# A one-core kernel of a two-layer selective-scan tower, attention and a quantised feed-forward: the later stages' steps placed inside the last iterations of the scan loop

## The chip, the cores and the metric

The kernel runs on one core of one Trainium2 chip. The metric is the device time of the program in microseconds (us), smaller is better. Before the change three runs took 442.88, 443.31 and 444.84 us; their median is 443.31. One more execution was profiled, and every row below is from that one.

## The reference, cut to what matters

Sixteen sequences of 128 tokens, 192 features each, fp32. Three stages follow one another, each with a residual:

```python
x = emb[input_ids]                                # (16, 128, 192)
for i in range(2):                                # selective scan block, inner width 384, 16 states
    x = x + mamba_block(rmsnorm(x, norm_w[i]), ...)
#   in mamba_block: xz = x @ in_proj_w; causal convolution of 4 taps, silu; x_dbl = xr @ x_proj_w;
#   delta = softplus(dt @ dt_proj_w + dt_proj_b); scan over the tokens; (y * silu(res)) @ out_proj_w
h = x
#   attention, 12 heads of 16: weights relu(1 + s + s*s/2) with s = q.k/4, divided by their sum
h = h + attention(layernorm(h)) @ w_proj + b_proj
#   feed-forward, 192 -> 2*512 -> 192: input and hidden are rmsnormed and rounded to 8 bits per token
#   (scale 127 / largest magnitude), weights rounded to -1, 0, 1; y = silu(gate) * up
h = h + bitlinear(y, w_out, g_out)
```

## The kernel before

The five engines run queues of their own and meet only at semaphores; the kernel is written by hand as one list of operations for each engine. A wait stands in the queue, so everything behind it on that engine waits too.

**The scan loop.** Work goes in eight chunks: two layers (`NL`) by four groups of four sequences (`NG`, `SG`), a chunk being 512 token columns, and the 384 inner channels three tiles `c` of 128 partitions. On each engine `for i in range(NJ + 5)` runs a software pipeline, in which iteration `i` handles different steps of chunks `i-1` to `i-5`. In the last iterations (`i` from 10 on) no new chunk comes in and the steps get fewer: `project_out(7, b)` of TensorE (L709) and `add_h(7, b)` of VectorE (L1273) end the loop. `gate(j, c)` (L1261) multiplies by the gate and releases `project_out(j)`. VectorE's part of a chunk is the convolution (L1172), `error` (L1164), `delta` (L1179), `input_times_b` (L1194), `memoryless_states` (L1208), the scan (L1200), `skip` (L1213), `times_c` (L1219). Whether the slower recurrence over 15 further states is needed is decided by a flag (L1266) that each engine reads (`states_*`); with these inputs the branch is not taken.

**Attention and feed-forward.** They start after the loop. `variances(g)` (L1280, L1283, L1285) of groups 0 to 2 stand in the last iterations of VectorE's loop, that of group 3 behind it; `normalise(s)` (L1369) follows. Per group of four sequences: `turn_x` (eight transposes, L763), `take_x` (L458, L461), `project_qk` twice (L776, L781), `take_q` and `take_k` (L470, L1376), `sum_tokens` (L1391), `sum_values` (L810), `project_v` (L792, L797), `take_v` (L1383). Per sequence, on TensorE: `scores` (L822), `values` (L836), `turn_sums` (L845), `turn_attention` (L851), `project` (L859), then of the feed-forward `turn_input` (L868), `project_up` (L882), `turn_hidden` (L891), `project_down` (L899). A second loop, `for i in range(SEQ + 6)`, issues one turn per sequence: attention of sequence `i` beside `project_up(i-3)`, `turn_hidden(i-4)` and `project_down(i-5)`. Between these steps ScalarE squares the scores (L478) and copies or applies silu (L487, L494, L501, L510, L516, L522), VectorE divides (L1406, L1411), adds (L1417) and finds the largest magnitudes (L1434, L1457), and GpSimd multiplies by the gain (L1044) and makes the scales.

**Banks and buffers.** There are eight PSUM banks. The loop uses 0 and 1 for transposes and for `project_out`, 2 to 7 for the rest. After it, the scores take 0 to 2, the pair 3 and 4 (`U_BANK`) holds in turn what `turn_x`, `project_qk`, `project_v` and `project_up` make, 5 is for values, 6 for attention, 7 for the feed-forward. The buffers of attention and feed-forward are views of the loop's buffers `pair` (xc, sz), `dl`, `du`, `arena` and `ring`; `pair`, `dl` and `du` are laid out with the channel tile outside and the chunk inside.

## Time and profile before

| | |
|---|---|
| median of 3 runs | 443.31 us |
| the profiled execution: its time | 447.74 us |
| its span, first to last instruction | 445.9 us |
| TensorE matmul busy | 382.3 us (86%), 1794 instructions |
| TensorE weight load busy | 203.9 us (46%) |
| VectorE busy | 324.2 us (73%) |
| ScalarE busy | 304.5 us (68%) |
| GpSimd busy | 202.0 us (45%) |
| mean granted TensorE clock | 0.891 of full speed |

Span and time differ by 1.84 us of start and end. The shares are means over stages with different limits: the scan loop (to about 259 us), the handover (to about 294), and attention with feed-forward. A matmul's end is modelled in the trace, since matmuls overlap; the distance between the starts of two steps is the safer measure.

### The profile page before, as it was taken

To read this page: it belongs to the slowest core of one execution; us is meant where nothing else is said; L and a number is where in the kernel's file an instruction comes from. 1 tells how busy PE (TensorE), PEld (TensorE's weight loads), DVE (VectorE), ACT (ScalarE), POOL (GpSimd) and SP (SyncE) were. 2 spreads that over 40 slices of the span, in tenths; PEclk is the share of its full clock that TensorE was granted. 3 is DMA by queue.
4 is the path that set the end of the run, shared out by engine and by line. 5 is a ranking of instruction groups with operands and counts; after the bars stand their busy time and mean duration, and the time that the engine had idled before them with its cause. 6 is when DMAs were issued, how large, how long until landed. Compare 5 with 4: busy or idle time off the path is not lost. (4 is left out here: it accounts for less than half of the span.)

```text
span 445.9 us, 6460 instructions
## 1 busy us (share of the span) xinstructions
PE 382.3 (86%) x1794; PEld 203.9 (46%) x1794; DVE 324.2 (73%) x687; ACT 304.5 (68%) x574; POOL 202.0 (45%) x298
## 2 busy tenths in 40 slices
PE   0489989999999999999887656989899999998853
PEld 0233333363444535445262551544665765665522
DVE  2079897999999999999979965134486477557752
ACT  1268997999999899998987002166296477558532
POOL 5546525355344543635254422002366445647772
PEclk9997895999999999999986666899699889989865
DMA  6832000000000000000000000000000000000000
GB/s 145 236 91 54 1 1 0 1 1 1 1 2 0 1 0 2 1 1 1 0 0 2 0 1 0 2 0 1 2 10 10 11 10 19 9 12 20 10 18 26
DMA packets 6877, 7.88 MB, mean 18 GB/s; under 512 B 1566, under 2 KB 5623, under 8 KB 6840
## 3 DMA queue, kind: packets, MB, share of 16 engines
q1 hardware_dynamic: 5238, 5.71, 4.6%
q0 software_dynamic: 768, 1.57, 1.6%
q8 instruction: 16, 0.26, 0.3%
q10 hardware_dynamic: 834, 0.17, 0.2%
q14 instruction: 21, 0.17, 0.1%
HBM read 5.87 MB, written 1.57 MB: 17 GB/s over the span
## 5 line engine op out<-in xcount | busy, mean ns | idle before, releaser
L583 PE MATMUL bank<-ring,win 96*128 96x512 f32 x192 | 101.4, 671 | 2.0 <-issue 1.2
L583 PEld LDWEIGHTS bank<-ring,win 96*128 96x128 f32 x192 | 37.4, 208 | 57.8 <-issue 52.0
L983 POOL TENSOR_TENSOR du<-dl,pair 128x512 f32<-128x512 f32 x24 | 30.9, 1289 | 71.8 <-DVE dmin L1179 71.8
L1172 DVE SCALAR_TENSOR_TENSOR pair<-bank,cw,pair 128x508 f32<-128x508 f32 (+2 forms) x72 | 52.2, 734 | 10.9 <-ACT pair L312 9.0
L709 PE MATMUL bank<-wout,pair 128*128 128x192 f32 x192 | 41.4, 376 | 5.9 <-DVE pair L1261 5.9
L709 PEld LDWEIGHTS bank<-wout,pair 128*128 128x128 f32 x192 | 37.1, 221 | 16.6 <-issue 9.1
L988 POOL TENSOR_TENSOR arena<-arena 128x512 f32<-128x512 f32 x24 | 30.6, 1274 | 30.9 <-DVE arena L1213 30.9
L977 POOL TENSOR_TENSOR arena<-arena,dl 128x512 f32<-128x512 f32 x24 | 30.5, 1269 | 14.8 <-DVE dl L1164 14.8
L478 ACT ACTIVATE pair<-bank 128x512 f32<-128x512 f32 x48 | 25.2, 597 | 11.1 <-PE bank L822 10.5
L637 PE MATMUL bank<-dbl,wdt 13*128 13x512 f32 x48 | 28.4, 675 | 4.6 <-issue 1.3
L1200 DVE TENSOR_TENSOR_SCAN arena<-arena 128x512 f32<-128x512 f32 x24 | 29.1, 1212 | 0.0
L312 ACT ACTIVATE pair<-bank,cb,cw 128x512 f32<-128x512 f32 x24 | 18.6, 774 | 13.6 <-PE bank L583 13.4
L1044 POOL TENSOR_TENSOR arena<-ring,gout 128x512 f32<-128x512 f32 x16 | 20.3, 1271 | 15.9 <-issue 10.1
L470 ACT ACTIVATE pair<-bank,parity 96x512 f32<-96x512 f32 x16 | 10.1, 678 | 22.1 <-PE bank L781 14.5
L620 PE MATMUL bank<-pair,wx 128*80 128x512 f32 x48 | 22.2, 599 | 2.3 <-ACT pair L346 2.2
L501 ACT ACTIVATE du<-bank,neg_rne 96x256 bf16<-96x256 f32 x16 | 7.5, 468 | 23.9 <-PE bank L868 23.9
L573 PE MATMUL bank<-ident,ring 128*96 128x128 f32 x64 | 9.2, 291 | 16.1 <-DVE ring L1150 16.1
L1179 DVE CUSTOM_DVE_ANT_0 dl<-du,arena 128x512 f32<-128x512 f32 x24 | 20.2, 843 | 1.4 <-ACT du L342 0.8
L342 ACT ACT_TABLE_LOAD x16 | 20.5, 1283 | 0.3
L959 POOL DMA_INDIRECT h<-emb,idx x16 | 17.7, 1108 | 6.0 <-issue 4.3
L776 PE MATMUL bank<-arena,wa 128*96 128x512 f32 x32 | 16.9, 655 | 3.0 <-ACT pair L470 1.6
L1164 DVE SCALAR_TENSOR_TENSOR dl<-du,dl 128x512 f32<-128x512 f32 x24 | 17.6, 734 | 2.5 <-ACT du L337 2.4
(161 smaller groups left out, 879.4 us busy)
## 6 DMA issues: line engine op xcount, KB each, us to landing
out<-h SPq DMA_DIRECT2D x16, 96.0 KB, 1.6
win<-in_w SPq DMA_DIRECT2D x2, 576.0 KB
arena<-ffn_in_t SPq DMA_DIRECT2D x1, 768.0 KB
wout<-out_w SPq DMA_DIRECT2D x2, 288.0 KB
arena<-ffn_out_t SPq DMA_DIRECT2D x1, 384.0 KB
wa<-w_qkv SPq DMA_DIRECT2D x1, 288.0 KB
wb<-w_qkv SPq DMA_DIRECT2D x2, 144.0 KB
h<-emb,idx POOLq DMA_INDIRECT x16, 6.9
```

The source lines that it names most:

```text
L342: nc.scalar.activation(du[:, c, j % NG, :], du[:, c, j % NG, :], ACT.Ln).then_inc(ln_done, 1)
L478: nc.scalar.activation(sq[:, s % 2, r, :], bank[:, r, :], ACT.Square, scale=HD ** -0.5, bias=1.0).then_inc(sq_ready, 1)
L583: last = nc.tensor.matmul(bank[:, b, :], win[:, j // NG, k, m * P:(m + 1) * P], xtr[:, j % 2, k, :], start=(k == 0), stop=(k == KH - 1))
L620: last = nc.tensor.matmul(bank[0:XM, XP_BANK, :], wx[:, j // NG, c, :], xc[:, c, j % NG, :], start=(c == 0), stop=(c == CI - 1))
L637: nc.tensor.matmul(bank[:, S_BANKS[c], :], wdt[DT_AT:DT_AT + R + 1, j // NG, c * P:(c + 1) * P], dbl[DT_AT:DT_AT + R + 1, j % 2, :], start ...
L709: last = nc.tensor.matmul(bank[:, T_BANK + b, i * D:(i + 1) * D], xc[:, c, j % NG, t0:t0 + LEN], wout[:, j // NG, c, :], start=(c == 0), s ...
L977: nc.gpsimd.tensor_tensor(relu_s[:, c, :], relu_s[:, c, :], dl[:, c, j % NG, :], ALU.subtract).then_inc(rest_done, 1)
L983: nc.gpsimd.tensor_tensor(du[:, c, g, :], dl[:, c, g, :], xc[:, c, g, :], ALU.mult).then_inc(du_ready, 1)
L988: nc.gpsimd.tensor_tensor(yv[:, c, :], yv[:, c, :], bx[:, c, :], ALU.add).then_inc(yv_done, 1)
L1044: nc.gpsimd.tensor_tensor(yg[:, s % SG, :], y[:, s % 2, :], gout[:, :], ALU.mult).then_inc(yg_ready, 1)
L1172: nc.vector.scalar_tensor_tensor(acc, seqs(bank[:, X_BANKS[c], :])[:, :, 0:LEN - tap], cw[:, j // NG, c, TAPS - 1 - tap:TAPS - tap], acc, ...
L1200: nc.vector.tensor_tensor_scan(bx[:, c, :], da[:, c, :], bx[:, c, :], 0.0, ALU.mult, ALU.add).then_inc(scan_done, 1)
```

## The change

There are three parts.

1. The layout of `pair`, `dl` and `du` becomes chunk outside, channel tile inside, so that a finished chunk leaves one contiguous slot. The views of attention and feed-forward are cut from such slots, and each first use waits for the loop's last use of its slot. The banks are renamed: scores 3, 5, 2, the shared pair 7 and 4, values 6, attention 0, feed-forward 1.
2. The loops stop early (ScalarE after iteration 10, TensorE after 9, GpSimd and VectorE after 7), and what is left is written out call by call, with steps of attention and feed-forward among those of the loop.
3. The second loop is gone too: all of its calls are written out in another order on each engine. Waits for banks leave the functions of TensorE and stand as single lines between the calls. The number of instructions of each kind is the same, except that GpSimd's two memsets of `va` become four, two for each half.

```diff
-U_BANK, PV_BANK, A_BANK, F_BANK = 3, 5, 6, 7
+U_BANKS, SC_BANKS, PV_BANK, A_BANK, F_BANK = (7, 4), (3, 5, 2), 6, 0, 1
...
-        pair = sb("pair", [P, 2, CI, NG, GT])
+        pair = sb("pair", [P, 2, NG, CI, GT])
...
+        q2 = q_view(sz_row, 0), q_view(dl_row, 2 * SLOT)
+        kk = k_view(sz_row, 4 * GT), k_view(dl_row, 2 * SLOT + 4 * GT)
+        va = v_view(dl_row, 0), v_view(du_row, 2 * SLOT)
+        xta = dl_row[:, SLOT:SLOT + GT], du_row[:, 3 * SLOT:3 * SLOT + GT]
+        xs = xsr
...
             def take_x(g):
+                if g == 0:
+                    act.wait_ge(scan_dve, 6 * DECAYING * DVE_U)
+                    act.wait_ge(du_ready, 18)
+                    act.wait_ge(da_ready, 18)
...
+            logarithm(7, 1)
+            states_act(6)
             take_x(0)
+            positive_part(7, 2)
+            decays(7, 0)
+            decays(7, 1)
+            silu_gate_in(7, 2)
+            logarithm(7, 2)
             take_q(0, 0)
+            decays(7, 2)
             take_q(0, 1)
...
             def project_up(s):
                 pe.wait_ge(qxt_ready, s + 1)
-                pe.wait_ge(y_done, s)
-                x, q, k, v = evicted(SG + s + 3)
-                pe.wait_ge(x_out, x)
-                pe.wait_ge(q_out, q)
-                pe.wait_ge(k_out, k)
-                pe.wait_ge(v_out, v)
...
+            pe.wait_ge(sz_ready, 23)
+            pe.wait_ge(dbl_ready, 8)
+            pe.wait_ge(bc_ready, 8)
             turn_x(0)
+            spread_b(7)
+            project_gate(7, 2)
+            states_pe(6)
+            pe.wait_ge(x_out, 3)
             project_qk(0, 0)
+            spread_g(7)
...
+            pe.wait_ge(y_done, 1)
+            project_v(1)
```

Three places show what moves. Each has the engine's order before, then after. Line numbers differ between the two files.

TensorE before, from the last `project_out` of the loop (L709) to the first steps of attention (L763 `turn_x`, L776 and L781 `project_qk`, L810 `sum_values`):

```order
L709 MATMUL bank<-wout,pair 128x192 x12
L763 MATMUL bank<-ident,arena 128x128 x4
L763 MATMUL bank<-ident,arena 64x128 x4
L776 MATMUL bank<-arena,wa 96x512 x2
L781 MATMUL bank<-arena,wb 96x512 x2
L776 MATMUL bank<-arena,wa 96x512 x2
L781 MATMUL bank<-arena,wb 96x512 x2
L810 MATMUL bank<-xsum,wvp 128x4 x6
```
TensorE after, in the iteration that handles chunk 7 (L911 and L916 are `project_qk`, L797 `spread_g(7)`, L803 `spread_c(7)`, L851 `project_out(6, b)`, L925 and L930 `project_v`):

```order
L911 MATMUL bank<-dl,wa 96x512 x2
L916 MATMUL bank<-dl,wb 96x512 x2
L797 MATMUL bank<-bc,not_first 128x512
L803 MATMUL bank<-dbl,picked 128x512
L911 MATMUL bank<-dl,wa 96x512 x2
L916 MATMUL bank<-dl,wb 96x512 x2
L851 MATMUL bank<-wout,pair 128x192 x6
L925 MATMUL bank<-wa,dl 128x192 x2
L930 MATMUL bank<-wb,dl 128x192 x2
L925 MATMUL bank<-wa,dl 128x192 x2
L930 MATMUL bank<-wb,dl 128x192 x2
L851 MATMUL bank<-wout,pair 128x192 x6
```
The first group's projections, which stood behind the whole loop, now stand before `project_out(6)` and `project_out(7)`, and `spread_g(7)` now stands behind the first of them.

VectorE before, from `gate(6, 0)` (L1261) over `error` and `delta` to `input_times_b(7, 1)` (the second L1194):

```order
L1261 TENSOR_TENSOR pair<-pair,arena 128x512
L1164 SCALAR_TENSOR_TENSOR dl<-du,dl 128x512
L1179 ISA dl,dmin<-du,arena 128x512
L1179 ISA dmin 128x1
L1194 TENSOR_TENSOR arena<-du,bank 128x512
L1208 TENSOR_TENSOR arena<-du,bank 128x512
L1194 TENSOR_TENSOR arena<-du,bank 128x512
```
VectorE after, the same stretch (L1819 gate, L1722 error, L1737 delta, L1752 `input_times_b`, L1766 `memoryless_states`):

```order
L1838 BN_STATS bst<-h 128x6 x4
L1841 BN_AGGR mv<-bst 128x2 x4
L1843 TENSOR_SCALAR ms<-mv 128x4
L1819 TENSOR_TENSOR pair<-pair,arena 128x512
L1722 SCALAR_TENSOR_TENSOR dl<-du,dl 128x512
L1737 ISA dl,dmin<-du,arena 128x512
L1737 ISA dmin 128x1
L1752 TENSOR_TENSOR arena<-du,bank 128x512
L1939 COPY pair<-bank 96x512
L1766 TENSOR_TENSOR arena<-du,bank 128x512
L1752 TENSOR_TENSOR arena<-du,bank 128x512
```
`variances(1)` (L1838, L1841, L1843) now stands ahead of `gate(6, 0)`, and `take_k(0, 0)` (L1939) between `input_times_b(7, 0)` and `memoryless_states(7, 0)`.

TensorE before, from the last `project` (L859) to the end (L891 `turn_hidden`, L868 `turn_input`, L899 `project_down`, L882 `project_up`):

```order
L859 MATMUL bank<-wp,du 128x192 x2
L891 MATMUL bank<-ident,arena 128x128 x4
L868 MATMUL bank<-ident,arena 96x128 x2
L899 MATMUL bank<-wq,du 128x192 x4
L882 MATMUL bank<-wq,du 128x512 x4
L891 MATMUL bank<-ident,arena 128x128 x4
L868 MATMUL bank<-ident,arena 96x128 x2
L899 MATMUL bank<-wq,du 128x192 x4
L882 MATMUL bank<-wq,du 128x512 x4
L891 MATMUL bank<-ident,arena 128x128 x4
L899 MATMUL bank<-wq,du 128x192 x4
L891 MATMUL bank<-ident,arena 128x128 x4
```
TensorE after, from the last `project` (L987) on (L994 `turn_input`, L1016 `project_down`, L1002 `project_up`, L1009 `turn_hidden`):

```order
L987 MATMUL bank<-wp,arena 128x192 x2
L994 MATMUL bank<-ident,ring 96x128 x2
L1016 MATMUL bank<-wq,arena 128x192 x4
L1002 MATMUL bank<-wq,arena 128x512 x4
L1009 MATMUL bank<-ident,pair 128x128 x4
L1016 MATMUL bank<-wq,arena 128x192 x4
L994 MATMUL bank<-ident,ring 96x128 x2
L1009 MATMUL bank<-ident,pair 128x128 x4
L1002 MATMUL bank<-wq,arena 128x512 x4
L1009 MATMUL bank<-ident,pair 128x128 x4
L994 MATMUL bank<-ident,ring 96x128 x2
L1002 MATMUL bank<-wq,arena 128x512 x4
```
Before, twelve steps of the feed-forward follow the last `project` (the last is not shown); now it is seventeen (eleven are shown), and `project_up` and `turn_hidden` of different sequences alternate.

## Rows read from the trace of the kernel before

**Rows 1.** Stages: window, length, busy us (instructions) per engine, PEclk, DMA share, GB/s.

```profile
232.57:258.76 26.19, 16.24 (x47) 10.12 (x45) 24.08 (x48) 10.37 (x13) 11.60 (x10) 0.63 0.00 1
258.76:269.43 10.67, 6.50 (x24) 6.23 (x24) 7.46 (x35) 0.00 (x0) 3.14 (x4) 0.77 0.00 1
269.43:294.20 24.77, 20.87 (x111) 10.67 (x111) 7.24 (x13) 8.17 (x16) 1.53 (x2) 0.79 0.00 1
294.20:398.00 103.80, 99.11 (x800) 62.38 (x801) 59.93 (x174) 64.44 (x150) 45.94 (x109) 0.92 0.03 9
422.04:445.90 23.86, 12.03 (x49) 7.03 (x47) 10.74 (x28) 7.01 (x15) 12.11 (x27) 0.57 0.06 21
```
**Rows 2.** Timeline, VectorE, end of the loop: start us, us, engine, line, operation, operands, count, idle before.

```profile
232.61 0.56 DVE L1273 TENSOR_TENSOR h<-h,bank 128x384 f32<-128x384 f32 x1 [2.50 <-PE bank L709]
...
252.33 1.12 DVE L1280 BATCH_NORM_STATS2 bst<-h 128x6 f32<-128x192 f32 x4
...
253.90 0.17 DVE L1285 TENSOR_SCALAR ms<-mv 128x4 f32<-128x4 f32 x1
...
256.86 1.90 DVE L1261 TENSOR_TENSOR pair<-pair,arena 128x512 f32<-128x512 f32 x3 [1.16 <-POOL arena L988]
```
**Rows 3.** Timeline, all engines, the handover's steps.

```profile
269.43 1.10 PE L763 MATMUL bank<-ident,arena 128*128 128x128 f32 x8 [3.97 <-DVE arena L1369]
...
270.13 0.60 ACT L458 ACTIVATE arena<-bank 128x512 f32<-128x512 f32 x1 [22.70 <-PE bank L763]
...
270.62 1.19 ACT L461 ACTIVATE arena<-bank 64x512 f32<-64x512 f32 x2
...
270.76 1.27 DVE L1391 TENSOR_REDUCE xsum<-arena 128x4 f32<-128x512 f32 x2
...
271.91 3.70 PE L776 MATMUL bank<-arena,wa 128*96 128x512 f32 x4 [1.38 <-issue]
...
277.63 0.69 DVE L1376 COPY pair<-bank 96x512 f32<-96x512 f32 x1 [5.03 <-PE bank L781]
...
288.40 1.02 DVE L1383 COPY pair<-bank 128x384 f32<-128x384 f32 x2 [4.09 <-PE bank L797]
...
289.33 0.37 DVE L1369 TENSOR_SCALAR arena<-h,mv,rstd 128x192 f32<-128x192 f32 x1
```
**Rows 4.** Timeline, TensorE, two turns with projections and a group's last turn.

```profile
373.69 1.14 PE L822 MATMUL bank<-pair 32*128 32x256 f32 x12
...
378.40 1.88 PE L776 MATMUL bank<-arena,wa 128*96 128x512 f32 x4
...
381.24 0.55 PE L845 MATMUL bank<-ident,ring 128*128 128x128 f32 x3
...
381.94 1.14 PE L822 MATMUL bank<-pair 32*128 32x256 f32 x12
...
386.70 1.92 PE L810 MATMUL bank<-xsum,wvp 128*128 128x4 f32 x12
...
388.55 0.92 PE L792 MATMUL bank<-wa,arena 128*128 128x192 f32 x4
...
389.93 1.55 PE L792 MATMUL bank<-wa,arena 128*128 128x192 f32 x4
```
**Rows 5.** Stage, one group of four sequences in the dense part.

```profile
333.24:369.87 36.63, 35.77 (x291) 22.90 (x289) 23.40 (x68) 23.61 (x56) 19.07 (x45) 0.91 0.04 12
```
**Rows 6.** Timeline, project_up and hidden of sequence 11; sequence 15 to the end.

```profile
407.84 1.03 PE L882 MATMUL bank<-wq,du 96*128 96x512 bf16 x4
...
410.24 0.75 DVE L1452 SCALAR_TENSOR_TENSOR ring<-bank,deq,ring 128x512 f32<-128x512 f32 x1
...
424.20 0.35 DVE L1417 TENSOR_TENSOR h<-h,bank 128x192 f32<-128x192 f32 x1
...
431.88 0.63 PE L868 MATMUL bank<-ident,arena 128*96 128x128 f32 x2 [1.31 <-issue]
...
443.48 0.42 DVE L1472 SCALAR_TENSOR_TENSOR h<-bank,deq,h 128x192 f32<-128x192 f32 x1 [2.87 <-PE bank L899]
```
## What I predict, before any run of the changed kernel

> **What bounds the kernel now.** I read the page's busy shares first (TensorE 86%), then the table of stages, then the timeline at the seams. No single engine bounds the whole. In the scan loop VectorE does: from 232.57 to 258.76 it is busy 24.08 of 26.19 us, TensorE 16.24 [rows 1]. Between 258.76, where the last gate ends [rows 2], and 269.43, where `turn_x(0)` starts, ScalarE is idle and VectorE does statistics and `normalise`. From 269.43 to 294.20 TensorE projects the first group in a bare chain: turn, copy, project, copy, project. The clock column says 0.79 there, and 0.63 in the stretch before the last gate [rows 1]. From 294.20 to 398 TensorE is busy 99.11 of 103.80 us, ScalarE 64.44, VectorE 59.93: TensorE bounds. In the last 23.86 us it is busy 12.03 at a clock of 0.57; the feed-forward chain of the last sequences bounds.
>
> To see whether a busy TensorE is really full I measured from start to start. A turn with one projection lasts 373.69 to 381.94, 8.25 us; the projection in it runs from 378.40 to 381.24, 2.84 us [rows 4]. A turn without it is thus 5.41 us. `sum_values` is 386.70 to 388.55, 1.85 us; half of `project_v` 388.55 to 389.93, 1.38 us, the whole 2.76 us; `turn_x` 1.10 us [rows 3, 4]. A group of four needs 4 x 5.41 + 2 x 2.84 + 1.85 + 2.76 + 1.10 = 33.0 us. It took 36.63 [rows 5], a factor of 1.11. The clock column there is 0.91 and busy is 35.77, so most of the excess is clock, not waiting.
>
> **Part 1: the handover.** I compare the two at one common point: the loop's `project_out(7, 1)` done, and of attention the whole projection of group 0, `turn_x(1)`, `scores(0)` and `(1)`, `values(0)` and `turn_sums(0)`. Before, that is 294.20. In the new TensorE queue exactly this set is complete when `project_out(7, 1)` ends. So I need the end of the last gate, and what follows it.
>
> The last gate ended at 256.86 + 1.90 = 258.76 [rows 2]. VectorE now has more in front of it. `variances(0)` was in front already (252.33 to 254.07, 1.74 us [rows 2]) and only goes earlier. New are `variances(1)`, 1.74; four `normalise`, 4 x 0.37 = 1.5; `take_k` twice, 2 x 0.69 = 1.4; `sum_tokens`, 1.27; `take_v`, 1.02 [rows 3]; `take_csum`, one small instruction, left out. That is 6.9 us. Two old holes take some of it: 2.50 us before 232.61, where VectorE waits for `project_out(5, 1)`, and 1.16 us before 256.86, where it waits for GpSimd [rows 2]. The first fills only in part, since `variances(0)` and `normalise(0)` stand so early that they also push the input of the TensorE step which is waited for; I count 1.1 of it, and all of the second. 6.9 - 2.3 = 4.6 us.
>
> Then there is a new wait. `take_k(0, 0)` stands in VectorE's queue before `memoryless_states(7, 0)`, and needs turn (1.10), ScalarE's copies (0.60 + 1.19) behind a table load, and `project_qk(0, 0)`; the latter is 2.84 us at full clock, and took from 271.91 to 277.63, 5.7 us, when it ran cold [rows 3, 4]. Also `spread_g(7)`, which `memoryless_states` needs, now stands behind that projection. Together 5.7 to 8.6 us, plus table load and spread. Beside it VectorE has six or seven instructions at about 0.65 (the gates take 1.90 / 3 [rows 2]) and `variances(1)`, about 6 us. The uncovered rest is between 0 and 6 us; no row shows it; I take 3.4, nearer to the cold end, as the clock is 0.63 in this stretch. What queues behind `take_k(0, 0)` is all the rest of chunk 7 on VectorE, so this wait goes fully to the last gate. Last gate: 258.76 + 4.6 + 3.4, about 266.8.
>
> Behind it TensorE has `project_out(7, 0)`, `turn_x(1)`, `turn_sums(0)`, `project_out(7, 1)`. The two `project_out` together took about 6.6 us at low clock before, 6.50 of TensorE's busy time in the window after the last gate [rows 1]; half to all of it now, plus 1.10 and 0.55, and I take 6.1 together. Common point: 272.9 instead of 294.20, a gain of 21.3 us. Bounds: 24.7 without the new wait; 16 if the wait is 6 us and everything else runs cold too. What carried the gain: TensorE's 20.87 us of the handover window now stand beside VectorE's chain, where TensorE was busy only 16.24 of 26.19.
>
> The views cut from finished slots and the new layout add no instruction and no work; I cost them at nothing. The waits on first use (say `du_ready` 18 before `take_x(0)`) are for steps of chunk 5 or 6, behind which the queues already stand. GpSimd's memsets (two more) lie where it is idle about half of the time [rows 1]. The scan loop's first seven iterations keep their order.
>
> **Part 2: the body.** TensorE work left at the common point: 16 turns of 5.41, less 3.5 for the steps already done, 83.1; group 1 without `turn_x` 10.3; groups 2 and 3 11.4 each. Sum 116.2 us at full clock. Seventeen feed-forward steps stand behind the last `project`; three are `project_up` at 1.03 us [rows 6], the others shorter than a turn's mean step of 0.6: about 8 us. So 108.2 us lie before it. I take the old factor of the dense part, 1.11: 120.1 us. The bounds are 1.02 (all at full clock, hardly a wait: 110.3) and 1.17, what the old order needed from 294.20 to 424.20 for its own 111 us of work (126.6). Since the dense part is already 1.11, a new order alone gives little there; it gains in the old turns 12 to 15, which have no projection to cover the chain.
>
> **Part 3: the tail.** From `add_attention(15)` at 424.20 to the end of the last addition, 443.90, are 19.7 us, and 2.0 more to the span's end for the store [rows 6]. In these 19.7 TensorE stood 1.31 us before `turn_input(15)` though its input was there, and ran at clock 0.57. The new queues have more to do in the same stretch (17 steps instead of 12), but no fixed turn. I take 17, with bounds 15 and 20.
>
> **Sum.** 272.9 + 120.1 + 17 + 2.0 = 412.0 us of span, against 445.9: 33.9 less, of which 21.3 is handover and 12.6 body and tail. The profiled execution took 447.74 for its span of 445.9; the median of the runs is 443.31. I subtract from the median: 443.3 - 33.9 = 409. Ends of all bounds: 269.5 + 110.3 + 15 + 2 = 396.8 and 278 + 126.6 + 20 + 2 = 426.6 of span, that is 394 and 424 as a time.
>
> **The rivals.**
> A. *Handover only.* The body and tail take what they took, 151.7 us from the common point. Time 443.3 - 21.3 = 422. For it: TensorE is busy 95% there, so there is little to fill. Against: the last turns and the tail have room [rows 1].
> B. *The clock.* If the mixed order is granted 1.2 GHz half of the time instead of the present share (mean 0.92 of 2.4 GHz, so about 16% of the time), then, by 2.84 against 5.7 us for the same projection, the rate falls from 0.92 to 0.75: 120.1 x 0.92 / 0.75 = 147, 27 us more: 436. Against it: stretches of low clock lie where TensorE waited, and it will wait less.
> C. *Slower: the shared pair of banks.* Every `turn_x`, `project_qk`, `project_v` and `project_up` writes the pair 7 and 4, and must wait until the last user is read out. After `project_up` that takes from 408.87 to 410.99, 2.1 us (silu, then `hidden`) [rows 6]; after `turn_x` 1.8, `project_qk` 1.3, `project_v` 1.0 [rows 3]. In the old order all of it lay beside other steps. If the written order puts these users where their covers have run out, 27 handovers cost 16 x 2.1 + 2 x 1.8 + 6 x 1.3 + 3 x 1.0 = 48 us: 409 + 48 = 457. It is slower than before from 34 of the 48 on, so if more than two thirds of them stand bare. Against it: in the new queue three or four steps stand between users nearly everywhere.
> D. *TensorE isn't the bound.* Its times overlap and are modelled; if they shrink when fed better, ScalarE is next, with 64.44 of 103.80. Body and tail would fall to about 110 in all: 272.9 + 110 + 2 = 385 of span, 382. Against: start to start distances, not modelled ends, gave 33.0 us for a group. The Trainium skill says the same as D in "Perfetto Trace Analysis", section "Identifying the Most-Contended Engine": matmul busy time misleads, and weight-load busy time and useful flops should be used. Weight loads are busy 22.90 of 36.63 us [rows 5], so by that rule there would be room and D's time would come out; I hold the distances between starts to be the better witness.
> E. *The handover mostly fails.* The new waits in VectorE's queue cost not 3.4 but about 15 us, since each of take_k, sum_tokens and take_k again meets a TensorE that isn't there yet. Gain 34 - 12 = 22: time 421.
>
> **How the numbers follow.** Forecast 0.60, 409, its own range 399 to 418. A 0.15, B 0.09, C 0.04, D 0.03, E 0.09. About 0.5%, 2.2 us, is what a measurement can tell from no change. All but C lie far below 443: faster 0.95, same 0.01, slower 0.04. The range of 8 in 10 reaches from 398 to 424: forecast, A and E are in it nearly whole, B, C and D are out.
>
> **What would show it.** In the changed profile: `project_out(7, 1)` ends near 273 (268 to 280); VectorE has a wait of 1 to 6 us before the first copy of k; the last gate is later than before, near 267; TensorE is over 90% busy from there to the last `project` near 393; the last addition follows `add_attention(15)` by 15 to 20 us. I am wrong if the last gate is behind 275 (E), if the body from the common point to the last `project` takes over 130 us (B by the clock row, C if waits stand before the users of banks 7 and 4), or if it takes under 105 us (D).

## The result: 428.9 us, faster, but outside the range that I gave

In the first comparison the changed kernel took 428.89 us (median of 4, 423.78 to 430.52), the kernel before 444.07 (442.88 to 446.28); the ratio is 0.9577, 95% interval 0.948 to 0.9674. Run again with six executions (e9 below) it took 423.6 us (421.9 to 427.9), ratio 0.9509 (0.9459 to 0.9558). All ten together have a median of 424.0. I had forecast 409, range 398 to 424.

### The profile after

The profiled execution took 423.78 us, its span is 422.0 (before: 447.74 and 445.9), so it is an average one of the ten. First its stages, with the columns of [rows 1]: end of the loop; wait for the last gates; last gates to `project_out(7, 1)`; body to `add_attention(15)`; tail to the last addition.

```profile
225.00:242.50 17.50, 14.63 (x58) 8.11 (x58) 14.00 (x36) 15.53 (x25) 9.21 (x8) 1.00 0.01 1
242.50:261.70 19.20, 16.57 (x82) 10.47 (x80) 16.68 (x31) 8.36 (x12) 6.51 (x6) 0.91 0.00 1
261.70:270.70 9.00, 8.84 (x73) 7.75 (x73) 5.71 (x19) 4.00 (x9) 0.00 (x0) 0.81 0.00 1
270.70:392.40 121.70, 115.12 (x980) 72.47 (x978) 77.93 (x233) 79.20 (x183) 61.58 (x145) 0.94 0.03 10
392.40:419.70 27.30, 15.77 (x63) 8.36 (x62) 13.20 (x33) 9.46 (x19) 15.70 (x36) 0.57 0.06 19
```
The row of 26.19 us in [rows 1] runs from `add_h(5, 1)` to the end of the last gate, with TensorE busy for 16.24 us; now the same stretch is 232.95 to 263.62 and TensorE is busy 26.27 of 30.67 us. In the last row it is busy 15.77 of 27.30, at a mean clock of 0.57 (0.50, that is 1.2 GHz, from about 396 us on).

VectorE's timeline (start, length, line, operation, idle before it in brackets) around the new wait and the last gates answers to [rows 2]:

```profile
240.33 0.68 DVE L1752 TENSOR_TENSOR arena<-du,bank 128x512 f32<-128x512 f32 x1
242.21 0.69 DVE L1939 COPY pair<-bank 96x512 f32<-96x512 f32 x1 [1.20 <-PE bank L916]
243.15 0.69 DVE L1766 TENSOR_TENSOR arena<-du,bank 128x512 f32<-128x512 f32 x1 [0.26 <-PE bank L797]
...
261.73 1.89 DVE L1819 TENSOR_TENSOR pair<-pair,arena 128x512 f32<-128x512 f32 x3
```
L1939 is `take_k(0, 0)`: it waits 1.20 us for `project_qk` in this execution (up to 5.15 us in others of the same code, see under e7). The last three gates (L1819) end at 263.62. TensorE behind them, where [rows 3] show the old handover:

```profile
261.87 0.86 PE L965 MATMUL bank<-du,dl 128*32 128x128 f32 x24 [0.33 <-DVE csum L1970]
262.66 1.92 PE L953 MATMUL bank<-pair 32*128 32x256 f32 x12
264.51 3.08 PE L851 MATMUL bank<-wout,pair 128*128 128x192 f32 x12
267.42 1.04 PE L902 MATMUL bank<-ident,ring 128*128 128x128 f32 x8
268.29 0.49 PE L973 MATMUL bank<-ident,arena 128*128 128x128 f32 x3
268.62 2.12 PE L851 MATMUL bank<-wout,pair 128*128 128x192 f32 x12
```
`values(0)` (L965) and `scores(1)` (L953) run while VectorE still gates, then come `project_out(7, 0)`, `turn_x(1)`, `turn_sums(0)` and `project_out(7, 1)`, without a gap, to 270.74. Before, this point was reached at 294.20.

Then the tail, which answers to [rows 6]. TensorE from the last `project` on; L1009 is `turn_hidden`, L1016 `project_down`, L994 `turn_input`, L1002 `project_up`:

```profile
391.52 0.89 PE L987 MATMUL bank<-wp,arena 96*128 96x192 f32 x4
393.19 0.39 PE L994 MATMUL bank<-ident,ring 128*96 128x128 f32 x2 [0.78 <-DVE ring L2021]
394.15 0.50 PE L1016 MATMUL bank<-wq,arena 128*128 128x192 bf16 x4 [0.56 <-ACT arena L528]
394.49 1.03 PE L1002 MATMUL bank<-wq,arena 96*128 96x512 bf16 x4
397.38 1.11 PE L1009 MATMUL bank<-ident,pair 128*128 128x128 f32 x4 [1.86 <-DVE h L2052]
399.36 0.80 PE L1016 MATMUL bank<-wq,arena 128*128 128x192 bf16 x4 [0.87 <-ACT arena L555]
400.99 0.63 PE L994 MATMUL bank<-ident,ring 128*96 128x128 f32 x2 [0.83 <-DVE ring L2021]
402.18 1.11 PE L1009 MATMUL bank<-ident,pair 128*128 128x128 f32 x4 [0.56 <-ACT arena L528]
...
412.72 1.11 PE L1009 MATMUL bank<-ident,pair 128*128 128x128 f32 x4 [0.87 <-DVE h L2052]
414.70 0.80 PE L1016 MATMUL bank<-wq,arena 128*128 128x192 bf16 x4 [0.87 <-ACT arena L555]
416.50 1.09 PE L1009 MATMUL bank<-ident,pair 128*128 128x128 f32 x4 [1.00 <-DVE pair L2046]
418.46 0.80 PE L1016 MATMUL bank<-wq,arena 128*128 128x192 bf16 x4 [0.87 <-ACT arena L555]
```
Read the brackets: nearly every step shown waits 0.6 to 1.9 us for another engine. `turn_input`, `turn_hidden` and `project_down` all write bank 1 (`F_BANK`), and L528, L555 and L2052 (`take_input`, `take_hidden`, `add_ffn`) read it out. Not all of these waits are for the bank: `round_input` (L2021) and `round_hidden` (L2046) make a step's own input, and what `take_hidden` copies is also the input of `project_down`. Read the lengths too: `turn_hidden` takes 1.11 us here, and 0.60 where the clock is full. And VectorE takes up sequence 15 late:

```profile
392.45 0.35 DVE L1992 TENSOR_TENSOR h<-h,bank 128x192 f32<-128x192 f32 x1
...
395.60 0.35 DVE L1996 BATCH_NORM_STATS2 bst<-h 128x6 f32<-128x192 f32 x1
...
401.35 0.41 DVE L2007 SCALAR_TENSOR_TENSOR ring<-h,mv,gin 128x192 f32<-128x192 f32 x1
...
419.29 0.42 DVE L2052 SCALAR_TENSOR_TENSOR h<-bank,deq,h 128x192 f32<-128x192 f32 x1 [2.94 <-PE bank L1016]
```
Its `input_stats` starts 3.2 us behind `add_attention(15)`, its `input_gain` 8.9 us.

Three stages, in us of the profiled executions, are what the rest of this text compares (before's common point is [rows 3]'s 294.20; the handover column is counted from the start of the first `project_out`, since the loop's start differs by 1 to 3 us between executions):

| kernel | first `project_out` to common point | body | tail | tail's clock | tail's matmuls | median of runs (range) |
|---|---|---|---|---|---|---|
| before | 203.6 | 130.0 | 19.7 | 0.59 | 41 | 443 to 446 (440.8 to 449.8) |
| changed | 181.4 | 121.7 | 27.3 | 0.57 | 63 | 428.9 (423.8 to 430.5) |
| e9 changed again | 183.9 | 118.5 | 27.3 | 0.57 | 62 | 423.6 (421.9 to 427.9) |
| e1 new handover, old loops | 183.9 | 125.5 | 19.6 | 0.59 | 41 | 424.3 (423.5 to 428.2) |
| e2 tail warm | 188.0 | 121.8 | 23.4 | 1.00 | 113 | 425.0 (420.3 to 428.4) |
| e3 tail banks | 188.0 | 121.6 | 24.8 | 0.64 | 62 | 428.6 (421.7 to 429.8) |
| e4 both | 188.1 | 118.6 | 22.6 | 1.00 | 108 | 424.1 (415.4 to 425.7) |
| e5 input 15 early | 188.1 | 121.6 | 28.3 | 0.57 | 62 | 432.2 (428.2 to 433.7) |
| e6 e4 and new order | 188.1 | 121.7 | 20.7 | 1.00 | 113 | 422.9 (416.6 to 426.0) |
| e7 handover warm | 184.5 | 118.5 | 27.3 | 0.57 | 62 | 424.8 (423.1 to 426.2) |
| e8 e6 and e7 | 184.4 | 121.8 | 21.0 | 1.00 | 113 | 421.0 (418.1 to 422.7) |
| e10 e1, e7's and e2's warming | 184.6 | 125.5 | 18.7 | 1.00 | 94 | 425.3 (423.4 to 426.5) |
| e11 scores late | 194.6 | 122.4 | 26.8 | 0.56 | 62 | 436.6 (425.9 to 438.3) |
| e12 less put off | 186.8 | 119.7 | 25.1 | 0.57 | 50 | 425.6 (419.1 to 431.0) |

(The 63 of the changed kernel counts one matmul of the last `project` that reaches into the window; 62 begin in the tail, and in the old order 40. The matmuls of e2, e4, e6, e8 and e10 include the added ones. The tail of unchanged code is the steadiest of the three stages: 27.3 us in the changed kernel, e9 and e7.) The ratios' intervals leave disturbed runs out, which for e3, e4, e6 and e12 keeps only two or three runs; there I go by the stages and by the medians of all runs. Against the ten executions' 424.0 none of e2 to e7 and e12 is clearly faster by its median, so what they gain is read from the tail alone.

### The profile page after: what moved, and what is told of

It reads as the page before. It is cut to its first block and busy times, and to the rows that moved or that the text cites. A ratio compares the mean times of both kernels' runs of the same rounds, so it can differ in the third digit from the quotient of the medians.

```text
span 422.0 us, 6474 instructions
## 1 busy us (share of the span) xinstructions
PE 368.7 (87%) x1794; PEld 194.7 (46%) x1794; DVE 320.8 (76%) x687; ACT 305.2 (72%) x574; POOL 200.3 (47%) x300
## 3 DMA queue, kind: packets, MB, share of 16 engines
q0 software_dynamic: 768, 1.57, 1.8%
HBM read 5.87 MB, written 1.57 MB: 18 GB/s over the span
## 5 line engine op out<-in xcount | busy, mean ns | idle before, releaser
L725 PE MATMUL bank<-ring,win 96*128 96x512 f32 x192 | 98.4, 652 | 3.1 <-issue 2.1
L499 ACT ACTIVATE du<-bank 128x512 f32<-128x512 f32 x48 | 25.1, 599 | 16.4 <-PE bank L953 16.3
L851 PEld LDWEIGHTS bank<-wout,pair 128*128 128x128 f32 x192 | 31.6, 194 | 10.8 <-issue 10.8
L851 PE MATMUL bank<-wout,pair 128*128 128x192 f32 x192 | 36.2, 340 | 0.0
L762 PE MATMUL bank<-pair,wx 128*80 128x512 f32 x48 | 23.6, 630 | 3.8 <-ACT pair L345 3.6
L1472 POOL TENSOR_TENSOR pair<-pair,gout 128x512 f32<-128x512 f32 x16 | 20.9, 1304 | 11.5 <-issue 7.5
L1002 PE MATMUL bank<-wq,arena 96*128 96x512 bf16 x64 | 18.2, 410 | 4.0 <-ACT arena L528 2.9
L1737 DVE CUSTOM_DVE_ANT_0 dl<-du,arena 128x512 f32<-128x512 f32 x24 | 19.7, 821 | 2.0 <-ACT du L341 1.9
L555 ACT ACTIVATE arena<-bank,neg_rne 128x512 bf16<-128x512 f32 x16 | 10.9, 684 | 13.2 <-PE bank L1009 12.9
L367 ACT ACTIVATE arena<-dl,decay 128x508 f32<-128x508 f32 x24 | 16.5, 713 | 4.4 <-DVE dmin L1737 4.3
L2032 DVE SCALAR_TENSOR_TENSOR pair<-bank,deq,pair 128x512 f32<-128x512 f32 x16 | 12.0, 748 | 8.5 <-ACT pair L539 5.9
```

The lines of the kernel that those rows point to most:

```text
L499: nc.scalar.activation(sq[s % 2][:, r, :], bank[:, SC_BANKS[r], :], ACT.Square, scale=HD ** -0.5, bias=1.0).then_inc(sq_ready, 1)
L725: last = nc.tensor.matmul(bank[:, b, :], win[:, j // NG, k, m * P:(m + 1) * P], xtr[:, j % 2, k, :], start=(k == 0), stop=(k == KH - 1))
L762: last = nc.tensor.matmul(bank[0:XM, XP_BANK, :], wx[:, j // NG, c, :], xc[:, j % NG, c, :], start=(c == 0), stop=(c == CI - 1))
L851: last = nc.tensor.matmul(bank[:, T_BANK + b, i * D:(i + 1) * D], xc[:, j % NG, c, t0:t0 + LEN], wout[:, j // NG, c, :], start=(c == 0), s ...
L1002: last = nc.tensor.matmul(bank[:, U_BANKS[half], :], qxt[:, s % 2, k, :], wq1[:, k, half * F:(half + 1) * F], start=(k == 0), stop=(k == K ...
L1472: nc.gpsimd.tensor_tensor(yg[:, s % SG, :], y[:, s % 2, :], gout[:, :], ALU.mult).then_inc(yg_ready, 1)
```

## The experiments

**e1: the handover alone.** The new queues up to `project_out(7, 1)`, then the old loop on each engine:

```
             project_out(7, 1)
-            pe.wait_ge(attn_ready, 1)
-            turn_attention(0)
-            ...   (the placed calls, to project_down(15))
+            for i in range(SEQ + 6):
+                g, part = i // SG + 1, i % SG
+                if 2 <= i < SEQ:
+                    scores(i)
+                if 5 <= i < SEQ + 5:
+                    ...
+                    project_down(i - 5)
```


> The changed kernel's handover up to project_out(7,1) of the last loop, and behind it the loops of the kernel before (one turn a sequence, its order and its waits on every engine). If the handover's gain is real and independent of what follows, project_out(7,1) ends near 271 us as in the changed kernel (before 294.2) and, with the old 151.7 us behind it, the span is near 422.5 and the median near 420 to 423: as fast as the whole change or faster by 1 to 2%. Theory S (the placed order of the body gains what the body of the changed kernel seemed to: 4 to 6 us, and its tail gives it back): body from 271 to the last project near 128 us (changed kernel 121.7 to add_attention(15)), tail from add_attention(15) to the last addition near 19.7 us (changed kernel 27.3). Rival (the handover only moves work that is paid back in the body, since the old turns then find nothing ready): body over 132 us and a median of 428 or more.

Measured: 424.3 us, just above the 420 to 423 I expected; ratio 0.9547 (0.9503 to 0.9591). The changed kernel's repeat has 0.9509 (0.9459 to 0.9558); the two can't be told apart. Its body and tail:

```profile
274.60:400.10 125.50, 118.28 (x1002) 75.14 (x1000) 82.17 (x244) 81.07 (x189) 68.17 (x157) 0.95 0.04 11
400.10:419.70 19.60, 9.86 (x41) 5.26 (x40) 8.75 (x23) 6.81 (x14) 10.91 (x23) 0.59 0.05 15
```
Against the changed kernel's rows: 1002 matmuls in the body instead of 980, and 41 in the tail instead of 63. The same work is done; the changed order puts 22 matmuls, ten VectorE and thirteen GpSimd instructions behind `add_attention(15)`. The body gets 3.8 us shorter (7.0 in e9) and the tail 7.7 us longer. So theory S holds: the handover is the gain, and placing the rest one by one gives back in the tail what it gains in the body.

**e2, e3, e4: clock and banks of the tail.** e2 adds, ahead of each wait of the tail, three matmuls into a bank that nothing reads:

```
+            def dummy(n=3):
+                for _ in range(n):
+                    nc.tensor.matmul(bank[:, SC_BANKS[2], 0:2 * D], wq2[:, 0, 0:P],
+                                     wq2[:, 0:2, :].rearrange(...), start=True, stop=True)
+            dummy()
             pe.wait_ge(h_out, 11)
             turn_hidden(11)
```
e3 gives the transposes banks of their own and drops the waits for the other users (the first of the waits; the rest of the tail likewise):

```
-  bank[:, F_BANK, c * P:(c + 1) * P]              (turn_hidden, take_hidden)
+  bank[:, SC_BANKS[1] if s >= 11 else F_BANK, c * P:(c + 1) * P]
-  bank[0:KP, F_BANK, k * P:(k + 1) * P]           (turn_input, take_input)
+  bank[0:KP, SC_BANKS[0] if s >= 14 else F_BANK, k * P:(k + 1) * P]
             project_up(13)
-            pe.wait_ge(h_out, 11)
             turn_hidden(11)
-            pe.wait_ge(yt_ready, 12)
+            pe.wait_ge(h_out, 11)
             project_down(11)
   ...
```


> The changed kernel, with three added matmuls of 384 columns on TensorE ahead of each of the 18 waits from project(15) on, into a bank that nothing reads any more; their results are read by nobody. If the tail's length is TensorE's clock (steps at 1.2 GHz: a turn_hidden's four transposes take 1.1 us instead of 0.6), the granted clock of the last 30 us rises from 0.66 to over 0.85 and the tail from add_attention(15) to the last addition falls from 27.3 to 21 to 24 us, so 3 to 6 us less (median near 424). If the tail is a chain through one shared PSUM bank or through VectorE's order, the clock may rise and the tail stays within 2 us of 27.3, or grows by the added matmuls that stand in the way (each set takes about 0.5 us at full clock, 1 us at half).

> The changed kernel, with the tail's transposes in banks of their own: turn_hidden and take_hidden of sequences 11 to 15 in a bank that the scores have left, turn_input and take_input of 14 and 15 in another, project_down alone keeps the feed-forward bank. If one bank shared by three kinds of steps makes the tail (theory B: 17 steps in turn, each waiting for the copy out of the one before), the tail falls from 27.3 to 19 to 22 us and the median to about 422. If the clock makes it (theory C), the steps still run at half speed and the tail is 25 us or more. If VectorE's order makes it (theory O: sequence 15's gain at 401.4 and its hidden rounding at 415.9 stand behind others' additions), the tail falls by 1 to 3 us at most.

> Both edits of the tail together: banks of their own and the added matmuls (results read by nobody). If bank chain and clock are both terms, the gains add up: tail 17 to 19 us, median near 419. If the one hides behind the other, it is as the better one alone (20 to 22 us). If VectorE's order is the bound, it stays over 24 us.

Measured, one row of the tail each (e2, e3, e4):

```profile
398.30:421.70 23.40, 18.04 (x113) 9.95 (x111) 13.56 (x33) 9.36 (x19) 15.46 (x35) 1.00 0.07 22
```
```profile
400.70:425.50 24.80, 14.69 (x62) 7.53 (x62) 13.17 (x33) 9.46 (x19) 15.67 (x36) 0.64 0.07 20
```
```profile
398.10:420.70 22.60, 16.87 (x108) 9.54 (x105) 13.22 (x33) 9.63 (x19) 15.61 (x36) 1.00 0.07 22
```
The clock alone is worth 3.9 us of tail, the banks alone 2.5, both 4.7: two terms that overlap. Each theory had part of it and neither all: with the bank chain gone at half clock 24.8 us are left, theory B had expected 19 to 22. In e4 TensorE's longest waits are for VectorE's rounding, not for a bank:

```profile
404.74 0.42 PE L994 MATMUL bank<-ident,ring 128*96 128x128 f32 x2 [1.24 <-DVE ring L2040]
...
408.48 0.63 PE L1009 MATMUL bank<-ident,pair 128*128 128x128 f32 x4 [0.55 <-DVE pair L2065]
```

**e5, e6: the order in the tail.** e5 moves three calls of sequence 15 on VectorE and one on GpSimd:

```
             add_attention(15)
+            input_stats(15)
+            input_gain(15)
+            largest_input(15)
             round_input(13)
   ...
             hidden_most(11)
+            input_root(15)
             gain(12)
```


> The changed kernel, with one thing moved: sequence 15's input_stats, input_gain and largest_input stand on VectorE directly behind add_attention(15) (in the changed kernel 3, 15 and 17 calls behind it), and input_root(15) on GpSimd ahead of gain(12). TensorE's order, banks and clock are as they are. Theory O (VectorE's order makes the tail): sequence 15's normalised input is there 5 us earlier and the tail from add_attention(15) to the last addition falls from 27.3 to 22 to 24 us. Theory B (TensorE's order through one shared bank at half clock): turn_input(15) still stands behind turn_hidden(13) in the same bank, so the tail moves by less than 1 us either way.

Measured: tail 28.3 us, 1.0 longer. (The 432.2 us of the whole owe only this 1.0 to the edit; in the profiled execution the rest lies ahead of the tail, in unchanged code.) Theory O in this form fell. The gain of 15 now runs at once, but `round_input(13)`, on which TensorE's next step waits, stands behind it:

```profile
401.38 0.35 DVE L1992 TENSOR_TENSOR h<-h,bank 128x192 f32<-128x192 f32 x1
...
402.45 0.42 DVE L2007 SCALAR_TENSOR_TENSOR ring<-h,mv,gin 128x192 f32<-128x192 f32 x1
402.91 0.35 DVE L2012 TENSOR_REDUCE amax<-ring 128x1 f32<-128x192 f32 x1
403.18 0.31 DVE L2021 TENSOR_SCALAR ring<-ring,step 128x192 f32<-128x192 f32 x1
```
The rounding (L2021) starts 1.80 us behind `add_attention(15)`; in the changed kernel 0.27. TensorE's `turn_input(13)` waits 2.29 us instead of 0.78, and the chain through the bank hands the loss on to the end.

e6 keeps banks and warming of e4 and lays out all four queues of the tail anew, with `turn_input` of 13 in the other bank too. TensorE's first steps, before (e4) and now:

```
-  project(15) turn_input(13) project_down(10) project_up(13) turn_hidden(11) project_down(11) turn_input(14)
+  project(15) project_down(10) turn_input(13) project_up(13) turn_input(14) project_up(14) turn_hidden(11)
```


> The kernel of e4 (tail transposes in banks of their own, added matmuls whose results nobody reads) with the tail of all four engines, from hidden(12) on, in another order: made from the durations of e4's trace so that sequences 14 and 15 get their input steps first. In e4 the tail took 22.6 us at a granted clock of 1.00; the same steps laid out with those durations and 0.1 us between engines come to 19 us. If order is the third term of the tail (theory O), the tail falls to 19 to 20.5 us; if what is left in e4 is the work of one engine or handing over between engines, it stays at 22 us or more.

Measured: tail 20.7 us; the order is worth another 1.9. 422.9 us, as e4's 424.1 within their spread. It still needs more than the old order's 19.6 at half clock, since it has half as much again to do; GpSimd is busy 15.43 us of it, about as much as in e2 to e4; whether GpSimd is what limits it now no run tests.

**e12: less work put off.** `turn_hidden(11)`, its copy, and `project_down` and `add_ffn` of 10 and 11 are replaced by their semaphore alone:

```
             def project_down(s):
                 pe.wait_ge(yt_ready, s + 1)
+                if s in (10, 11):
+                    pe.sem_inc(dn_ready, 1)
+                    return
```


> The changed kernel, leaving out the last feed-forward steps of sequences 10 and 11 that the old order has ahead of add_attention(15) and the changed one behind it: turn_hidden(11), take_hidden(11), project_down and add_ffn of 10 and 11 (12 of the 22 matmuls by which the changed tail exceeds the old one; those two sequences come out without their feed-forward term). Theory P (work put off makes the tail long: each such step stands in the chain through the one bank): these steps take the chain from 397.0 to 401.0 us in the changed kernel's trace, so the tail falls from 27.3 to 23 to 24 us and the median from about 424 to about 420. If the put-off steps only fill waits of the chain of sequences 12 to 15, the tail stays within 1.5 us of 27.3.

Measured: tail 25.1 us, 2.2 shorter; between the two expectations (4 and under 1.5). About half of the time of these steps was on the path: 0.18 us for each of the 12 matmuls left out. Where they stood, `turn_input(14)` now waits 3.12 us for VectorE's rounding:

```profile
404.02 0.63 PE L997 MATMUL bank<-ident,ring 128*96 128x128 f32 x2 [3.12 <-DVE ring L2030]
```

**e7, e8, e9, e10: the clock at the handover, and everything together.** e2 to e6 have the changed kernel's code up to the tail, yet they all took 188 us to the common point where its profiled execution took 181.4. Where this goes (232 to 248 us), the changed kernel and e3:

```profile
232.00:248.00 16.00, 12.39 (x40) 5.26 (x39) 12.60 (x29) 14.71 (x20) 7.31 (x6) 0.93 0.01 2
```
```profile
232.00:248.00 16.00, 15.51 (x37) 9.41 (x36) 8.52 (x23) 13.03 (x18) 7.71 (x7) 0.52 0.01 2
```
TensorE is granted 0.93 in the one and 0.52 in the other, and does the same steps in more time. `take_k(0, 0)` on VectorE waits for one of them, here in e9 and in e3 (L1937 is the same call):

```profile
244.50 0.69 DVE L1939 COPY pair<-bank 96x512 f32<-96x512 f32 x1 [2.73 <-PE bank L916]
```
```profile
249.32 0.69 DVE L1937 COPY pair<-bank 96x512 f32<-96x512 f32 x1 [5.00 <-PE bank L916]
```
The wait is 1.20 us in the changed kernel's profiled execution, 2.73 in e9 and 5.00 to 5.15 in e2 to e6. Counted from the first `project_out`, the last gate ends after 174.4, 175.8 and 180.9 to 181.0 us. So some 3.8 to 3.9 of the 6.7 us between the shortest and the longest are this one wait, which is longest where the clock is lowest. Ahead of this stretch the changed kernel and e3 have the same idle gaps on TensorE (1.37, 0.77 and 1.27 us between 219 and 231). e7 fills them:

```
             spread_c(6)
+            pe.wait_ge(xt_ready, 15)
+            pe.wait_ge(h_added, 9)
+            warm(6, T_BANK)
             project_x(7)
+            warm(4, T_BANK)
             project_steps(7, 0)
             project_out(5, 0)
             project_steps(7, 1)
+            pe.wait_ge(xt_ready, 16)
+            pe.wait_ge(h_added, 10)
+            warm(6, T_BANK + 1)
             project_steps(7, 2)
   ...
             project_out(6, 0)
+            pe.wait_ge(h_added, 12)
+            warm(12, T_BANK + 1)
             pe.wait_ge(q_out, 4)
```


> The changed kernel, with added matmuls of 384 columns (results read by nobody) in the idle gaps of TensorE at the handover: 6 ahead of project_x(7), 4 ahead of project_steps(7,0), 6 ahead of project_steps(7,2), 12 ahead of project_v(0). They cost up to 4.5 us of TensorE where it is idle for 1.4, 0.8, 1.3 and 3.1 us. Four traces of the same code up to here show project_out(7,1) ending 181.4, 188.0, 188.0 and 188.1 us behind the first project_out: the long ones have 14 to 16 us at 1.2 GHz after the gaps at 221 to 231 us, the short one does not. Theory K (these idle gaps let the clock fall, and that is the spread between runs): that distance is 181 or less, the granted clock from 221 to 275 us is over 0.95, and the median falls by 4 to 6 us to about 424. Rival (the clock falls whatever stands in the gaps, or the added work costs as much as it gives): distance 186 to 190, median unchanged near 428.

> All together: the handover's added matmuls, the tail's banks, added matmuls and new order. If the terms add up: 428.9 less 5 (handover clock) less 5 (tail banks and clock) less 3 (order) is near 416 us, 6 to 7% under the kernel before. If the handover's part fails, near 421.

> The changed kernel itself, once more, on the same chip as e10 and e11, for its median and its spread: 429 if the profiled run of 423.8 was a lucky one (its stretch from the first to the last project_out was 181.4 us; four others of the same code took 188.0 to 188.1), 424 if it was the rule.

> The kernel of e1 (new handover, old loops behind it) with the handover's added matmuls of e7 and three added matmuls ahead of each TensorE step of the tail (results read by nobody). Theory P (placing body and tail one by one brought nothing; the tail of the changed kernel is long because 63 matmuls stand behind add_attention(15) where the old order leaves 41): tail 16.5 to 18 us (e1 19.6 at a granted clock of 0.59), body 125, handover steady; median 419 to 421, level with e8, which needs the placed body, banks and a new tail order for it. If placing does bring something, e10 is 3 us or more behind e8's 421, at 424 or more.

Measured: e7 184.5 us to the common point, 424.8 us. The gaps are filled (0.28 us of idle time is left before `project_x(7)` instead of 1.37). The time to the common point is 3.5 less than in e2 to e6 and lies between the two expectations; but e9, the changed kernel with nothing added, also took only 183.9 and 423.6 us. Theory K fell: the added work shows no gain over the kernel's own repeat; the clock stays full to 236 us and falls then, with and without the added matmuls. The median of about 424 that I had expected of theory K came out, but by luck. That the six runs of e7 lie within 3.1 us and the ten of the changed kernel within 8.6 may be its doing or the chip's; that stays open.

e9 answers its question: the profiled 423.8 was not a lucky run; the first comparison's 428.9 was the high end of a spread.

e8: 421.0 us (418.1 to 422.7), ratio 0.9469 (0.9418 to 0.9521), the shortest median of the table and what I had expected if the handover's matmuls bring nothing. (The shortest single executions are e4's 415.4 and e6's 416.6, which no trace shows.) Against the changed kernel's 0.9509 in another comparison the intervals overlap: better by 2 to 3 us, probably, not shown.

e10: 425.3 us, a miss for theory P. The old order's tail hardly depends on the clock: 18.7 us at 1.00, 19.6 at 0.59, where I expected 16.5 to 18. (Its last added matmuls run on behind the last step and cost 2 us more to the span's end.) Its median is 4.3 us behind e8's, which I had set as the sign that placing the calls does bring something. But of the two profiled executions' difference of 2.3 us only 1.6 lie in the three stages, the ratios' intervals (0.9499 to 0.9580 against 0.9418 to 0.9521) overlap, and part of the rest is those last added matmuls. So that placing brings something once the tail's banks, clock and order are mended is likely, not shown.

**e11: the scores put back.** The projection of group 0 stays early; `scores(0)`, `sum_values(0)`, `values(0)`, `scores(1)`, `turn_x(1)` and `turn_sums(0)` go behind `project_out(7, 1)`:

```
-            scores(0)
             states_pe(7)
-            ...
             project_out(7, 0)
             project_out(7, 1)
+            scores(0)
+            sum_values(0)
+            values(0)
+            scores(1)
+            turn_x(1)
+            turn_sums(0)
```


> The changed kernel with one part of the handover undone: scores(0), sum_values(0), values(0), scores(1), turn_x(1) and turn_sums(0) stand on TensorE behind project_out(7,1) as in the kernel before, and square_scores(0) and take_csum(0) behind the last states and gates; group 0's projection stays early. If this part fills TensorE's wait for the last gates (theory F: these steps take 5 to 6 us of TensorE beside the gates), project_out(7,1) itself ends 2 to 4 us earlier but the common point (all of these done) comes 4 to 6 us later, and the median goes up by 4 to 6 us. If the wait for the gates was covered by other work anyway, or the gates come earlier by as much, it stays within 1 us.

Measured: `project_out(7, 1)` ends 184.8 us behind the first `project_out`, no earlier than in e9, and the common point comes at 194.6, 10.7 later than in e9. TensorE now waits for the gates with nothing in front of it, then does the rest in a row:

```profile
263.44 0.72 PE L832 MATMUL bank<-below,ones 128*128 128x1 f32 x6
267.63 5.82 PE L851 MATMUL bank<-wout,pair 128*128 128x192 f32 x24 [3.47 <-DVE pair L1819]
273.38 1.14 PE L953 MATMUL bank<-pair 32*128 32x256 f32 x12
274.45 1.95 PE L941 MATMUL bank<-xsum,wvp 128*128 128x4 f32 x12
```
Five of six runs took 435 to 438 us, one 425.9, which I can't explain. Theory F has the direction right and half of the size: besides TensorE's own work the chains to ScalarE and VectorE behind it (`turn_attention(0)` waits 1.57 us) now stand in the open. In this trace the part is thus worth up to half of the handover's 20 us: of the 10.7 us, 3.1 lie ahead of the end of the last gate, where the clock was low again (`take_k(0, 0)` waits 3.73 us), and 7.6 behind it. The trace is of one of the five long executions (granted clock 0.912); the short one, at 0.942, is only 2.3 us above e9's median. The direction is read from the steps in the trace, the size is not shown.

## Why the prediction was wrong

Step by step, against the profiled execution:

| step | predicted | measured |
|---|---|---|
| wait before `take_k(0, 0)` | 3.4 (0 to 6) | 1.2; 2.7 in e9, 5.0 to 5.2 in e2 to e6 |
| last gate ends | 266.8 | 263.6; 266.2 in e9, 269.4 to 272.7 in e2 to e6 |
| common point | 272.9 (268 to 280) | 270.7; 274.3 in e9, 276.5 to 279.8 in e2 to e6 |
| body, with the time to `add_attention(15)` | 120.1 | 121.7; 118.5 in e9 |
| tail | 17 (15 to 20) | 27.3 in both |
| to the span's end | 2.0 | 2.3 |
| span | 412.0 | 422.0; 422.1 in e9 |

- **Right: the handover.** Gain 23.5 us by the trace (predicted 21.3), 22.2 if both are counted from the first `project_out`; so counted it is 19.7 in e9 and 15.5 to 15.6 in e2 to e6. That one execution came out so near to 21.3 is partly luck; the range held for all. e1 shows the gain on its own. The new wait is there, between 1.2 and 5.2 us with the clock, as the prediction had it (0 to 6); rival E's 15 us fell.
- **Right: the body.** The factor 1.11 over the full-clock work gave a time within 1.7 us of the body in the changed kernel and in all of e2 to e9. Body and tail took 149 us, not about 110, so rival D fell; rival B's loss of clock didn't come (0.94 to 0.97). Of rival C next to nothing is there: TensorE waits 0.3 to 0.7 us before seven `project_up`, for five of them not for the pair of banks 7 and 4 but for ScalarE's copy of their own input (L528). One term was too small: the seventeen steps behind the last `project`, taken as about 8 us, are 10.3 us by their lengths at full clock (`turn_hidden` 0.60, `project_down` 0.49, `turn_input` 0.42, `project_up` 1.02).
- **Wrong: part 3, the tail.** "The new queues have more to do in the same stretch (17 steps instead of 12), but no fixed turn. I take 17." I saw that there was more work and forecast less time. The steps put off from the body were costed at nothing. Measured 27.3, a miss of 10.3 us, as much as the whole span's 10.0. In the old order the tail was 41 matmuls in 19.6 us; the new one has 63. What they cost is set by a chain of steps over four engines: one bank for three kinds of steps (2.5 us by e3), half clock (3.9 by e2), the order on all engines (1.9 by e6, behind the other two), overlapping one another. With all three mended 20.7 us are left, so no run of this order reached 17. Work by the durations of [rows 4, 5] could not show that; the tail of [rows 6] at a clock of 0.57 could have: at that tail's rate, 19.7 us for 41 matmuls, 63 would be 30, an upper estimate, since e12 shows only about half of such steps' time on the path. That is already far from 17.
- **Wrong: how the span became a median.** I took the difference between a predicted span and that of one profiled execution, which at 447.74 us was itself 4.4 us above the median of the three runs, and subtracted it from that median. The span with what lies around it, 412.0 + 1.8 = 413.8, was what the working gave. So 4.8 us of the miss is this, and 10.0 the span (tail 10.3 and end 0.3 more, body 1.6 more, handover 2.2 less): 409 + 4.8 + 10.0 = 423.8, the profiled execution; the ten runs have 424.0. The three runs' 443.3 was itself low: later medians of the kernel before, of four to eleven executions, are 444.1 to 446.3.
- **Rival A** came near in its number, 422, and not in its mechanism. It had body and tail at 151.7 us as before; they are 151.3 from the common point to the span's end. But they didn't stay as they were: body 8.3 us shorter, tail 7.6 longer. (Of the 8.3, 4.5 are in e1's old loops too, which run behind the new handover at a better clock, 0.95.)

What stays open: why one execution of e11 took 425.9 us, what limits the last 20.7 us of e6's tail, and what makes the clock fall at one point in one execution and at another in the next.

## To carry over

When a change shortens a dense stretch by reordering, count what stands behind the last step of the critical chain before and after: work put off into a sparse tail costs up to the tail's rate, here 0.35 us a matmul (7.7 us for 22; 0.18 for the twelve that e12 leaves out) where the body takes 0.12 (121.7 for 980). A tail is a chain through whatever its steps share, so give each kind of step its own bank there before placing its calls. Before taking a predicted difference from a median, see how far the profiled execution behind it lies from that median. And read a wait in more than one execution: the same wait was 1.2 us in one and 5.2 in another.

## What I had not expected of the hardware

**The same code falls to half clock at different points.** Up to the tail the changed kernel and e2 to e6 and e9 are one program, and took 181.4 to 188.1 us from the first `project_out` to the common point, and 118.5 to 121.8 for the body, with the granted clock at 0.52 to 0.93 in the same 16 us. The Trainium skill says in "TensorE: Matmul & The Clock Gate", section "Part 1: The HAM clock gate", that what watches the activity doesn't start anew with the kernel, so that the point of a change differs between runs. These traces agree that the point differs, from 181.4 to 188.1 us for one stretch; why, no run here shows. A gain of 3 to 4 us in the median is thus within what the place of a cold stretch makes.

**It also falls while TensorE never waits.** In the changed kernel, from 312 to 326 us:

```profile
312.00:326.00 14.00, 14.00 (x93) 9.03 (x92) 6.68 (x21) 6.75 (x15) 6.08 (x16) 0.76 0.03 9
```
TensorE is busy 14.00 of 14.00 us and is granted 0.76. It had just done `sum_values` (twelve matmuls with four columns each, 1.95 us for them):

```profile
312.46 1.95 PE L941 MATMUL bank<-xsum,wvp 128*128 128x4 f32 x12
314.34 1.11 PE L1009 MATMUL bank<-ident,pair 128*128 128x128 f32 x4
```
In e9 the same `turn_hidden` behind it still has the full clock, and the fall is shorter:

```profile
314.55 1.85 PE L941 MATMUL bank<-xsum,wvp 128*128 128x4 f32 x12
316.33 0.66 PE L1009 MATMUL bank<-ident,pair 128*128 128x128 f32 x4
```
e9's body is 3.2 us shorter at a clock of 0.97 instead of 0.94. All fourteen profiled executions bear the order of events out: between 295 and 390 us the clock falls 28 times in them, and each fall begins between 1.1 us before and 1.8 us behind the end of a `sum_values`. But nine of their 42 `sum_values` of groups 1 to 3 have no fall so near, and `project_v` and `project_qk` stand near them too. That the small matmuls make the clock fall is my guess; no run takes them away.

**Added matmuls hold the clock in the tail.** Three of 384 columns ahead of each wait of the tail lifted the granted clock from 0.57 to 1.00 and made the tail 3.9 us shorter, although each set takes TensorE 0.65 us; the median of e2, 425.0, doesn't show the gain. In the old, looser tail (e10) the same brought only 0.9.
